# The directed phase of a four-layer graph kernel: where the tensor engine's small steps stand

## The reference, cut to what matters

```
u     = h @ h.T / sqrt(D)
a     = softmax(u);  delta = a * adj;  attn = delta / (sum(delta) + 1e-10)
hl, hs, hr = h @ wl.T + b_l,  h @ ws.T + b_s,  h @ wr.T + b_r
ctx   = (attn * upper) @ hl + diag(attn) * hs + (attn * lower) @ hr
h     = relu(layernorm(ctx) * g + beta)
```

## Time and profile before

| what | us |
|---|---|
| median of three runs | 2835.5 (2833.78 to 2835.51) |
| the profiled execution, its own time | 2832.26 |
| its span, from the first to the last instruction | 2830.4 |
| PE busy in the span | 2698.6 (95%) |
| PE weight loads, DVE, ACT, POOL busy | 2340.6, 1771.4, 1249.9, 1092.4 |

### The profile page before, as it was taken

The page is one execution under the profiler, slowest core; times in us unless marked ns, Lnnn a source line. Parts: engine busy times, 40 slices in busy tenths (PEclk is TensorE's granted clock), DMA queues, the critical chain, the costliest instruction groups (busy, mean ns, idle before and its releaser), DMA issues. The chain is left out here.

```text
span 2830.4 us, 75501 instructions
## 1 busy us (share of the span) xinstructions
PE 2698.6 (95%) x29582; PEld 2340.6 (83%) x29582; DVE 1771.4 (63%) x4003; ACT 1249.9 (44%) x2180; POOL 1092.4 (39%) x1081
## 2 busy tenths in 40 slices
PE   6999999977999999999959999999999969999998
PEld 5888888866888888888848888888888868888887
DVE  6777777754545545554446787787877765566564
ACT  3444444434444444444423343343343325565564
POOL 1433433332322322332232443544444443545455
PEclk9999999998999999999979999999999989999999
DMA  4222222124112212211121111111111112222221
GB/s 138 72 70 70 69 66 65 58 72 126 32 56 78 67 33 67 77 31 56 49 89 36 49 61 39 56 55 49 50 50 49 49 52 72 85 92 73 89 84 59
DMA packets 186658, 183.15 MB, mean 65 GB/s; under 512 B 79568, under 2 KB 186064, under 8 KB 186576
## 3 DMA queue, kind: packets, MB, share of 16 engines
q1 hardware_dynamic: 186576, 181.99, 20.8%
HBM read 131.61 MB, written 50.33 MB: 64 GB/s over the span
## 5 line engine op out<-in xcount | busy, mean ns | idle before, releaser
L52 PE MATMUL l_psW<-w_hi,l_hT_hi 128*128 128x384 f32 x1920 | 678.0, 353 | 0.0
L52 PE MATMUL l_psW<-w_hi,l_hT_lo 128*128 128x384 f32 x1920 | 647.0, 337 | 0.0
L52 PE MATMUL l_psW<-w_lo,l_hT_hi 128*128 128x384 f32 x1920 | 644.6, 336 | 0.0
L52 PE MATMUL l_psW<-l_hT_hi,w_hi 128*128 128x512 f32 (+1 forms) x1242 | 490.7, 395 | 12.9 <-ACT l_m L1236 3.9
L52 PE MATMUL l_psW<-l_hT_hi,w_lo 128*128 128x512 f32 (+1 forms) x1242 | 469.6, 378 | 0.0
L52 PE MATMUL l_psW<-l_hT_lo,w_hi 128*128 128x512 f32 (+1 forms) x1242 | 468.8, 377 | 0.0
L52 PEld LDWEIGHTS l_psW<-w_hi,l_hT_hi 128*128 128x128 f32 x1920 | 361.8, 188 | 34.4 <-issue 24.6
L52 PEld LDWEIGHTS l_psW<-w_lo,l_hT_hi 128*128 128x128 f32 x1920 | 362.6, 189 | 0.7
L52 PEld LDWEIGHTS l_psW<-w_hi,l_hT_lo 128*128 128x128 f32 x1920 | 361.3, 188 | 0.0
L52 PEld LDWEIGHTS l_psW<-l_hT_hi,w_hi 128*128 128x128 f32 x1242 | 235.7, 190 | 75.9 <-issue 22.1
L284 POOL TENSOR_TENSOR l_s_d<-l_s_b,l_mx 128x768 f32<-128x768 f32 x128 | 188.7, 1474 | 240.2 <-DVE l_mx L562 185.4
(11 more groups left out here) (160 smaller groups left out, 5137.5 us busy)
## 6 DMA issues: line engine op xcount, KB each, us to landing
after_l<-l_xr SPq DMA_DIRECT2D x192, 192.0 KB, 1.9
l_xl<-after_l SPq DMA_DIRECT2D x47, 768.0 KB, 4.6
l_xr<-after_l SPq DMA_DIRECT2D x32, 768.0 KB, 4.5
l_xl<-in_x SPq DMA_DIRECT2D x16, 768.0 KB, 5.2
l_xr<-in_x SPq DMA_DIRECT2D x64, 192.0 KB, 2.4
l_xr<-after_l SPq DMA_DIRECT2D x64, 192.0 KB, 2.3
out_x<-l_xr SPq DMA_DIRECT2D x64, 192.0 KB, 2.0
l_adj<-in_adj SPq DMA_DIRECT2D x48, 128.0 KB, 2.4
```

The source lines that it names most:

```text
L52: last = nc.tensor.matmul(out, lhs[a](c), rhs[b](c), start=(m == 0), stop=(m == n - 1))
```

## The change

`delta_transposes` moves on PE from behind `right_part(u, 0)` to behind `right_part(u, 1)`, and `passed(above, 0)` follows it at once, ahead of `self_part(u, 0)` and no longer behind it. `passed(above, 1)` moves from behind `left_part(u, 2)` to directly behind `context(u, 0)`. `passed(above, 2)` stays. The results of `delta_transposes` go to the free columns 384 to 511 of the two banks `psC`. The wait for `dT_set` moves from `self_part(u, 0)` to the first `context`, there as a `wait_apart`. On DVE `left_copy(u, 1)` and `attention_sides(u)` change places.

```diff
     u_ps = psU[:, 0:TILES * NODES].rearrange("p (t n) -> p t n", t=TILES)
-    dT_ps = [x[:, TILES * NODES:TILES * NODES + PAIR * NODES].rearrange("p (t n) -> p t n", t=PAIR) for x in (psU, psT)]
+    dT_ps = [psC[:, odd, D:D + PAIR * NODES].rearrange("p (t n) -> p t n", t=PAIR) for odd in range(PAIR)]
...
             row_sums(u)
             if below is not None:
                 context_norm(below, 1)
+            left_copy(u, 1)
             attention_sides(u)
-            left_copy(u, 1)
...
                 pe.wait_ge(right_read, n + x)
-            if x == 0:
-                pe.wait_ge(dT_set, u.n + 1)
-            elif x == 2 or x == 1 and not is_first(u):
+            if x == 2 or x == 1 and not is_first(u):
                 pe.wait_ge(c_set, n + x - x % 2)
...
             n = u.n
+            if p == 0:
+                wait_apart(dT_set, n + 1)
             wait_apart(right_set, n * TILES + PAIR * (p + 1))
...
             right_part(u, 0)
-            delta_transposes(u)
             left_part(u, 1)
             right_part(u, 1)
+            delta_transposes(u)
+            if above is not None:
+                passed(above, 0)
             if first:
                 pe.wait_ge(w_lo_set, SELF + 1)
             self_part(u, 0)
-            if above is not None:
-                passed(above, 0)
             self_part(u, 1)
             context(u, 0)
-            left_part(u, 2)
             if above is not None:
                 passed(above, 1)
+            left_part(u, 2)
             right_part(u, 2)
```

## The result

The changed kernel takes 2845.38 us (median of 7 runs, 2841.21 to 2846.83), the kernel before 2833.78 us (7 runs, 2831.41 to 2835.67). The ratio is 1.0038, with a 95% interval of 1.0028 to 1.0047: 0.4% slower. The profiled executions stand at 2842.47 and 2832.26 us, their spans at 2840.4 and 2830.4.

A forecast was written before the change was run, and what follows sets the result against it. PE is always busy, but DVE's unbroken chain sets long units' end. 13 x 1.4 = +18.2, 17 x 0.2 = -3.4, unit 0 -3.2: +11.6 on 2832.26 gives 2843.9; median 3.2 higher, so 2847 us, range 2837 to 2857.

The forecast's parts named there:

- PE's lead in a long unit is used up: In the 13 units with both extras, DVE's 15.4 us without a hole sets the end; PE is 0.12 us early.
- rival A: POOL works off its colliding steps during DVE's wait; statistics start at 1837.8, PE leads everywhere, total 2824.7 us; chance 0.08.
- `result` 1.56 us late: On DVE in unit 13, `result` behind `attention_sides` starts at 1836.48 and not at 1834.92.
- The four steps behind it: delay shrinks to 1.42: Two `result` and two `row_factors` on DVE take turns with POOL; statistics start at 1839.95, not 1838.53.
- Rival B, half is caught up: Overlap and holes leave 0.5 to 0.8 us of delay a long unit, 2835.4 to 2839.3 us; chance 0.12.
- Rival C, the clock falls in the new stall: `self_part(u, 3)` runs at 1.2 GHz, its nine matmuls 1.56 us longer in 13 units, total 2867 us; chance 0.03.
- PE waits twice for `left_copy`: In long units PE's weight load waits at `self_part(u, 2)` and `self_part(u, 3)`, about 20 us in all.
- Merges 0.1 each: On PE, putting two small steps side by side saves 0.1 us a merge, 0.2 us a unit; bounds 0 and 0.25.
- The exit of 0.1: On PE, leaving a small step for projection matmuls costs about 0.1 us beyond its own work; merging pays it once.
- Unit 0: 3.2 us, up to 4.2: 18 projection matmuls fill 3.1 us of PE's 5.47 us wait for `delta`; 3.2 with one merge, 1 more by clock.
- Second register wait 0: The `wait_apart` added on PE before the context costs 0, at most 0.1 us in units where PE leads.

The follow-up runs named there:

- e1: Changed kernel with its two merges undone (`passed(above, 0)` and `passed(above, 1)` back in their old places), delta transposes still late; ratio 1.0049 to the kernel before.
- e2: Changed kernel with `delta_transposes` back behind `right_part(u, 0)`, `passed(above, 0)` directly behind them, and DVE's old order, keeping the merges; 2831.25 us.
- e4: Changed kernel with the statistics of long units moved on DVE to between `attention_sides` and the two `result` steps; 2826.37 us.
- e7: Kernel before with `delta_transposes` moved behind `right_part(0, 1)` in unit 0 alone; ratio 0.9998 to the kernel before.
- e3: Changed kernel with DVE's old order, `attention_sides` ahead of `left_copy(u, 1)`; 2846.59 us.
- e6: Changed kernel with the statistics moved on DVE ahead of `left_copy(u, 1)`, into the waits of 0.85 and 1.43 us; ratio 0.9964 to the kernel before.
- e8: e7 with the delta transposes' results in `psC` and the wait for `dT_set` at the context; ratio 0.9983 to the kernel before.
- e5: Changed kernel with the two `result` steps moved on DVE ahead of `attention_sides`, into the wait for `dT_done`; 2829.14 us.

## Why the prediction was right

The forecast was 2847 us and 0.4% slower, with a range of 2837 to 2857; measured were 2845.38 and 0.38%. The mechanism came as forecast: the late `dT_set` delays everything behind `attention_sides` on DVE, and PE waits for `left_copy`, in the 13 long units only. The sizes in the sum were less good, term by term:

- *PE's lead in a long unit is used up.* Right for the kernel before and for the change (e1). Too general as I put it: e2 shows that the bound moves with POOL's timing. I also had PE only 0.12 us early; a long unit was 0.23 above a short one, since a projection that had to wait is followed by 0.28 (1849.88 to 1850.16) and not 0.17. Only rival A used the 0.12.
- *`result` 1.56 us late.* Measured 1.59.
- *The four steps behind it: delay shrinks to 1.42.* Measured 1.20. The turns came as described, POOL's steps at 1.33 and 1.21 us; the four steps took 3.22 us, where I had worked out 3.47. This term was 0.2 us too large, 13 x 0.2 = 2.6 us in the sum. That the collision with POOL is real, and no property of the steps, is shown by e4 (and by line 1994 in e2).
- *Rival A, POOL makes way.* It didn't. e4 shows what it would have needed: a DVE step that doesn't collide in front. *Rival B, half is caught up:* the delay was 1.20 and not 0.5 to 0.8.
- *Rival C, the clock falls in the new stall.* The granted clock stayed at 1.00. Its price was also too high: at the lower level a projection matmul starts every 0.32 us (e7), so nine would have lost 1.3 us and not 1.56.
- *PE waits twice for `left_copy`.* 26 weight loads, 21.6 us, as forecast (about 20).
- *Merges 0.1 each.* Measured 0.065 (25.57 to 25.44 for two). The exit of 0.1 is saved, but transposes directly behind a 64*64 step take 0.42 (1835.95 to 1836.37) and not 0.35; these rows alone leave 0.04 to 0.05, and they are rounded to 0.01.
- *Unit 0: 3.2 us, up to 4.2.* Measured 4.64 in the change, 3.05 to 3.2 in e1 and e3 to e6. The wait fell to 2.67 us (forecast 2.4). The 1.4 to 1.6 us between the two are the clock, see below, and the forecast had allowed at most 1 us for it. That e7 failed shows a part of the edit that I had costed at nothing: without moving the wait for `dT_set` from `self_part` to the context unit 0 gains 0.4 us, with it 2.9 (e8).
- *Second register wait 0.* e8's short units of 25.57 with it and the earlier trace rows without it agree.

In the sum, the long units' loss was put 2.6 us too high and unit 0's gain 1.4 us too low, and the merges' gain 1.2 us too high: +11.6 forecast, +8.8 in the trace. The profiled executions lie 10.2 us apart: 1.4 more fell behind unit 31's start, where the forecast has nothing and where the other kernels' traces differ by up to 2.4 us with no pattern. The medians of seven lie 11.6 us apart; runs of one kernel differ by 5.6 us here and by 7.5 in e7, so that agreement to the decimal is luck. So is a part of the 2847: it was reckoned from a median of three runs, 2835.5, where seven give 2833.78.

## What to carry to other kernels

Before moving a step on the bounding engine, look at who starts on its result and what stands behind that wait in *its* order; the same 1.4 us wait cost nothing in 17 units and 1.2 us in 13. In the 15 even ones DVE had idle time behind it. In units 1 and 29 it had none up to the last `left_copy` either, but less work there, so PE still didn't wait. When such a wait is wanted for another reason, put work into it that depends on nothing late; of two candidates take the one that doesn't collide with a neighbour engine. (e6's 25.44 against e5's 25.69 points this way but doesn't isolate it, since e6's step is longer and also fills the hole of 0.85 us.) And a step's duration in a profile can belong to its neighbour: compare the same line in another stretch before moving it.

## What the runs showed of the hardware

DVE steps with both inputs in SBUF and POOL's tensor steps take turns, one whole instruction each: a 4-column DVE step lasts 0.15 or 0.97 us depending on when it comes, and POOL's 1.01 becomes 1.33. The Trainium skill's page "SBUF — State Buffer", section "Who interferes with whom", says that a DVE instruction with two SBUF inputs contends with a GpSimd instruction that reads SBUF, over ports that work as an exclusive lock, and that the order of issue decides who blocks. The traces agree, and statistics with one input ran beside POOL at an unchanged 1.93 us (e4), as the same section says of steps with at most one.

PE's clock behind unit 0's wait was not the same in kernels with the same order there. After idling 2.67 us in the change the projections behind the transposes start 0.17 to 0.18 us apart from the second on, at a granted clock of 1.00 (2.4 GHz); in e4, after 2.29 us, they start like this, 0.32 apart, at a granted clock of 0.50 (1.2 GHz):

```profile
1497.41 0.70 PE L2194 MATMUL l_psC<-ident,l_delta 64*64 64x64 f32 x16 [2.29 <-DVE l_delta L1977]
1498.04 1.11 PE L2163 MATMUL l_psT<-ident,l_rows 128*128 128x128 f32 x4
1498.81 0.67 PE L52 MATMUL l_psW<-w_hi,l_hT_hi 128*128 128x384 f32 x1
1499.27 0.52 PE L52 MATMUL l_psW<-w_lo,l_hT_hi 128*128 128x384 f32 x1
1499.59 0.52 PE L52 MATMUL l_psW<-w_hi,l_hT_lo 128*128 128x384 f32 x1
```

This is the 1.5 us between unit 0's 29.26 and 30.7 to 30.85 in the kernels e3 to e6. In e3 and e5, after 3.41 and 3.37 us, the delta transposes still took 0.39 us as at full clock, and only the projections behind them were slow. What decides it in a given execution these runs don't settle. The stalls of 0.9 us in the long units, by contrast, left the granted clock at 1.00 in all 13.
